# Attention and a quantised FFN on one core: key units on pairs of PSUM banks, another order at both ends of the loop, and seven blocks at once in the down stage

## What is computed

```python
x = x + xattn(_layernorm(x), ctx, ctx, mask, Wq, Wk, Wv, Wo)
    # q, k = rope(x Wq), rope(ctx Wk); logits = 30 tanh(q k * 0.0884 / 30); softmax; (w v) Wo
x = x + ffn(_layernorm(x), w1, w2, w3)
    # w -> NF4_CODE[searchsorted(bounds, w / absmax)] * absmax; (silu(x w1') * (x w2')) w3'
```

## Time and profile before

| | us |
|---|---|
| median of 3 runs (856.88 to 857.13) | 856.96 |
| profiled execution | 855.72 |
| span of its trace | 853.9 |
| TensorE busy | 803.7 |
| VectorE busy | 684.7 |
| GpSimd busy | 497.8 |
| ScalarE busy | 465.5 |
| mean granted clock of TensorE | 0.982 |

### The profile page before, as it was taken

One profiled execution on the slowest core, in us unless ns is written; L12 is line 12 of the kernel. 1 busy time (PEld: TensorE's weight loads), 2 busy tenths in 40 slices (PEclk: granted clock), 3 DMA queues, 4 the chain that ended last, 5 costly groups with the idle time before them and its releaser, 6 DMA issues.

```text
span 853.9 us, 10691 instructions
## 1 busy us (share of the span) xinstructions
PE 803.7 (94%) x3806; PEld 644.9 (76%) x3806; DVE 684.7 (80%) x745; ACT 465.5 (55%) x571; POOL 497.8 (58%) x270
## 2 busy tenths in 40 slices
PE   6798997999999999999999999998879999995998
PEld 4677885777788778877787778776668788884886
DVE  3876862589989899989989889889858999999512
ACT  5014752665665765665666656656325686866410
POOL 2545154776985986978977978967200344544100
PEclk9999998999999999999999999999999999997999
DMA  9676646432343433442533533412301121302112
GB/s 330 192 196 185 188 102 188 133 99 75 109 132 75 125 116 87 124 120 71 167 87 77 157 83 96 132 38 72 108 0 50 50 93 50 117 26 59 55 35 99
DMA packets 63541, 91.76 MB, mean 107 GB/s; under 512 B 6784, under 2 KB 30464, under 8 KB 63488
## 3 DMA queue, kind: packets, MB, share of 16 engines
q1 hardware_dynamic: 62304, 88.25, 35.7%
q10 hardware_dynamic: 1184, 2.82, 0.9%
HBM read 51.00 MB, written 19.07 MB: 82 GB/s over the span
## 4 chain that ended last, share of the span: by engine, by line
PE 81%; DVE 11%; issue 3%; DMA 2%; POOL 1%; ACT 1%; SPq 1%; DVEq 0%; POOLq 0%
PE bank L508 7%; PE bank L510 7%; PE bank L509 7%; PE bank L524 7%; PE bank L526 6%; PE bank L525 6%; PE avp L598 6%; PE bank L570 6%; PE bank L490 5%; PE bank L492 5%; PE bank L491 5%; PE trp L497 4%; DVE nfv L927 2%; PE bank L699 2%; PE bank L700 2%
## 5 line engine op out<-in xcount | busy, mean ns | idle before, releaser
L1247 POOL TENSOR_TENSOR eb<-eb,maskf 128x512 f32<-128x512 f32 x64 | 100.8, 1575 | 60.6 <-ACT eb L801 60.6
L799 ACT ACTIVATE eb<-bank 128x512 f32<-128x512 f32 x64 | 38.2, 597 | 177.6 <-PE bank L570 177.6
L1190 POOL TENSOR_TENSOR qT<-cs_loop,sw 128x512 f32<-128x512 f32 x57 | 101.9, 1787 | 34.8 <-DMA sw<-cs_loop 34.5
L508 PE MATMUL bank<-xh,wqh 128*128 128x512 f32 x256 | 106.5, 416 | 1.2 <-POOL wql L1181 1.2
L524 PE MATMUL bank<-woh,ath 128*128 128x512 f32 x256 | 107.6, 420 | 0.0
L526 PE MATMUL bank<-woh,atl 128*128 128x512 f32 x256 | 101.5, 396 | 0.0
L510 PE MATMUL bank<-xh,wql 128*128 128x512 f32 x256 | 101.5, 396 | 0.0
L525 PE MATMUL bank<-wol,ath 128*128 128x512 f32 x256 | 101.2, 395 | 0.0
L509 PE MATMUL bank<-xl,wqh 128*128 128x512 f32 x256 | 101.2, 395 | 0.0
L927 DVE SCALAR_TENSOR_TENSOR nfv<-nfq,nfv 128x1408 f32<-128x1408 uint8 x42 | 85.5, 2037 | 0.7
L935 DVE TENSOR_TENSOR cs_loop<-bank,csq 128x1024 f32<-128x1024 f32 x57 | 69.1, 1213 | 18.8 <-PE bank L510 18.8
(11 more groups left out here) (150 smaller groups left out, 1983.7 us busy)
## 6 DMA issues: line engine op xcount, KB each, us to landing
sw<-cs_loop SPq DMA_DIRECT2D x114, 128.0 KB, 2.3
stage<-wq_pieces SPq DMA_DIRECT2D x32, 256.0 KB, 3.0
stage<-wo_pieces SPq DMA_DIRECT2D x32, 256.0 KB, 2.8
stage<-dq_scratch SPq DMA_DIRECT2D x32, 256.0 KB, 3.6
sw<-cs_start SPq DMA_DIRECT2D x46, 128.0 KB, 2.3
ks_scratch<-qT SPq DMA_DIRECT2D x16, 256.0 KB, 2.5
vs_scratch<-vst SPq DMA_DIRECT2D x16, 256.0 KB, 3.2
kcur<-ks_scratch SPq DMA_DIRECT2D x16, 256.0 KB, 2.9
```

The lines of the kernel that those rows point to most:

```text
L508: nc.tensor.matmul(o, wqh[:, g, k, :], xh[:, k, cs], start=k == 0, stop=False)
L1190: nc.gpsimd.tensor_tensor(dst, products(ru, slot)[:, 0, :], sw[:, slot, :], ALU.add).then_inc(roped, 1)
```

## The change

The banks of `prj` become one tensor `prjs` of two banks. A key unit now writes the first bank of a pair, `prjs` or `avp` in turn. ScalarE copies its halves of 64 partitions crosswise into the second bank (`key_swap`), VectorE multiplies both banks by the two tables at once (`key_parts`), GpSimd subtracts (`key_rope`); SyncE sends no swaps for key units. The low parts of pieces 5 and 7 stand ahead of the first products on VectorE, those of 8 to 19 stand on GpSimd, and ScalarE's high parts stand between the copies.

SyncE issues the first four weight pieces of the loop during value units 14 and 15 and stores chunk 0 behind the loads of keys and values; ScalarE makes the first high part behind the tanh of step 1. From step 57 on `out_unit(j - 1)` stands ahead of the transposes of step j, and the work of the last head is spread anew over its steps. `nf_before` puts 122 places into the loop (116 before), 43 into the hidden units 0 to 19 (50 over all 22 before), and the rest behind the first pass of the down stage. In the down stage seven blocks go at once, into `lgp` too, so that the transposes of w3 have `trp` alone but for the second; one block follows.

```diff
+        key_pair = [prjs, avp]
...
-        FIRST_POOL = (0, 3, 6, 8, 10, 16, 18, 20, 22, 24, 26)
+        FIRST_POOL = (0, 3, 6, *range(8, 20), 20, 22, 24, 26)
...
             if slot <= NSTEP:
-                return 2 * min(max(0, slot - 2), 58)
+                return 122 * min(max(0, slot - 2), 58) // 58
             if slot <= NSTEP + 2 * HT:
-                return 116 + 50 * (slot - NSTEP) // (2 * HT)
-            return min(166 + 2 * (slot - NSTEP - 2 * HT), 16 * 11)
+                return 122 + min(43 * (slot - NSTEP) // 20, 43)
+            return min(165 + 2 * (slot - NSTEP - 2 * HT), 16 * 11)
...
+            def key_swap(u):
+
+                act.wait_ge(proj_done, u + 1)
+                pair = key_pair[u % 2]
+                nc.scalar.activation(pair[0:64, 1, :], pair[64:128, 0, :], ACT.Copy)
+                nc.scalar.activation(pair[64:128, 1, :], pair[0:64, 0, :], ACT.Copy).then_inc(key_swapped, 1)
...
+            def key_parts(u):
+
+                dve.wait_ge(key_swapped, u + 1)
+                wait(dve, roped, u - 1)
...
+                    key_pair[u % 2][:, :, :].rearrange("p c (b t) -> p c b t", b=4),
...
-            for n in (0, 3, 6):
+            for n in (0, 3, 6, 8):
                 first_low(n)
...
-                rope(u, u % 2, qT[:, u % 8 // 4, u % 4, :])
-                for n in {0: (8,), 2: (10,), 12: (16,), 13: (18,)}.get(u, ()):
-                    first_low(n)
-                if u == 5:
+                key_rope(u, qT[:, u % 8 // 4, u % 4, :])
+                if u < 7:
+                    first_low(u + 9)
+                if u == 7:
                     power(0, range(B))
+                if 11 <= u < 15:
+                    first_low(u + 5)
...
+                if v >= 14:
+                    head_piece(2 * v - 28)
+                    head_piece(2 * v - 27)
...
             weights(0)
+            weights(1)
             high(32)
-            weights(1)
...
+                    alone = j + AHEAD >= NUNIT
+                    if alone:
+                        out_unit(j - 1)
+                    if last and b in (3, 4):
+                        weight_transposes(b - 3)
+                    if last and b in (5, 7):
+                        token_transposes(b - 5)
+                        token_transposes(b - 4)
                     pe.wait_ge(an_done, j + 1)
...
-                    if j > 0:
+                    if j > 0 and not alone:
                         out_unit(j - 1)
...
-                for b in range(6):
+                for b in range(7):
+                    if n == 0 and b == 6:
+                        pe.wait_ge(wt_lo, 2 * HT + 2)
                     last = down(b, n, outs[b])
...
+                if n == 2 * HT - 1:
+                    down_hi(0)
...
-                for c, i in nf_adds(NSTEP + 2 * HT + n):
+                for c, i in nf_adds(NSTEP + 2 * HT + n - 1) if n > 0 else ():
                     nf_add(c, i)
```

205 lines of the change are left out of this document (108 added, 97 removed).

## The result

| | kernel before | changed kernel |
|---|---|---|
| median of the runs, us | 857.05 (856.88 to 858.10) | 830.35 (829.30 to 830.96) |
| span of the profiled execution, us | 853.9 | 828.9 |
| mean granted clock over the span | 0.982 | 0.994 |

The ratio is 0.9685, with a 95% interval of 0.9668 to 0.9701: 3.15% faster, 26.7 us. The forecast was 832.2 us in a range of 821 to 843.

What follows compares the result with a forecast made beforehand. TensorE was taken as the bound, busy 803.7 of 853.9 us, leaving about 39 idle us to win. Terms -7.5, -3.7, -7.4, -11.2 and +5.0 make -24.8: span 829.1, median 832.2 us, range 821 to 843.

Steps and rivals of the forecast that it cites:

- The sum: Whole kernel: five terms, -7.5 - 3.7 - 7.4 - 11.2 + 5.0, give -24.8 us on the profiled span.
- the steady loop: Loop from 152.3 to 580 us, where TensorE is never idle: nothing to gain, with 2 us as a bound for added adds.
- Key units: Key units up to the value stage: ScalarE copies replace the DMAs, value stage near 61.6 instead of 69.11, -7.5 us.
- The chain of a bank pair: Key units: a pair of banks is held 5.45 us against 5.46 TensorE needs for two units, so it just fits.
- the new wait of unit 8 on piece 15: Key unit 8: TensorE waits about 3.1 us for piece 15's low part on GpSimd, with 1.5 of half clock behind.
- The price of the copies: Key units: two ScalarE copies cost 1.09 us, bounds 1.0 and 2.4; rival of dear copies, 841 us, chance 0.10.
- Entry: Entry of the loop: earlier weight pieces and conversion behind the tanh start the unit at 147.0 instead of 152.30, -3.7 us.
- Loop's end: Last seven steps: output product ahead of transposes and spread layer norm start the first gate product near 629.7, -7.4 us.
- each after a wait of 0.9 to 1.6, under the limit of the clock: Loop's end: output products of steps 57 on wait only 0.9 to 1.6 us, so the clock doesn't fall.
- Gap: Before the down stage: no adds in the last two hidden units, start at 775.1 instead of 783.86, -11.2 us with clock.
- New wait in the down stage: Down stage: later last adds delay piece 8 to 814.5, wanted at 811.2; +3.3 us and +1.7 half clock, +5.0.
- the one on waits and the clock: Every TensorE wait: no loss of clock up to 1.8 us, a loss from about 2.

Runs made afterwards that it cites:

- low32_first: Changed kernel with GpSimd making the low part of piece 32, the first new query weight, ahead of the dequantization's multiply; 827.41 us, ratio 0.9639 to the kernel before.
- third_add_55: Changed kernel with the dequantization's places rounded otherwise, so a third add falls at step 55 and not at step 59; 828.26 us, ratio 0.9650 to the kernel before.
- places_before_b: Changed kernel with the dequantization's places as in the kernel before (116 in the loop, 50 in the feed-forward stage); 836.12 us, ratio 0.9741 to the kernel before.
- keys_alone_b: Kernel before with only the key units' part of the change (paired banks, two ScalarE copies, new order); 850.27 us, ratio 0.9914 to the kernel before.
- the last kernel: Changed kernel with piece 32's low part earlier, third add at step 55, 44 feed-forward places, piece 11's low part on VectorE, mask tables over two units; 816.42 us.
- low15_on_dve: Changed kernel with the low part of context piece 15 made on VectorE behind key unit 5, not on GpSimd; 829.62 us, ratio 0.9665 to the kernel before.

## Why the prediction was right, and where its steps were off

The sum was -24.8 us on the span and the measured one is -25.0. Where the waits would stand, and on what, is borne out below, but that the sum hits to 0.2 us is luck: the terms are off by +0.8, -0.3, +0.9, +0.2 and -2.2, and the steady loop, put at nothing, by +0.4. Of the -2.2, 1.7 are a half clock that stayed away in this execution and came in five of the six others that have the same wait.

**Key units, -7.5 said, -6.7 measured.** The chain of a bank pair (5.45 us for 5.46) was right, as the run with a third copy shows, and so was the new wait of unit 8 on piece 15. Two things were not in the walk. The operations on the mask tables, which I had costed at nothing, slow down beside GpSimd and make unit 6 wait 1.15 us:

```profile
22.95 1.09 DVE L998 TENSOR_TENSOR maskf<-maskf,nomask 128x128 f32<-128x128 f32 x1
23.95 1.38 DVE L999 TENSOR_TENSOR csq<-tab,keep 128x128 f32<-128x128 f32 x1
```

so unit 8 started 1.0 us later than said (34.89 for 33.9). And the units with transposes, 10 to 15, take 20.4 us together (42.04 to 62.47), where 2.73 + 0.36 + 0.1 for each makes 19.1: another 1.3, 0.4 of it one wait for VectorE's products. So the value stage started 2.4 us later than said (63.99 for 61.6). On the other side its first wait is 1.52 and not 2.02, and the half clock behind it went, 1.6 us that I had not counted. The price of the copies, for which I had bounds of 1.0 and 2.4 us, came out at 1.15. The rule of the Trainium skill (ScalarE: Activation LUTs, Step-by-step: what each stage is for), that ScalarE writes PSUM faster than SBUF, is borne out by 0.01 us only in the run with a third copy: 0.57 against 0.58 for the same shape.

**Entry, -3.7 said, -4.0 measured.** The wait was forecast at 2.9 us on GpSimd's order multiply, then low part; it is 2.57, and low32_first shows that order to be its whole cause. Of the gain, 2.7 us are SyncE's earlier issue.

**Loop's end, -7.4 said, -6.5 measured.** Less the 10.3 us won before it, my starts of the output products are 582.8, 589.0, 596.8, 603.2, 609.2 and 614.2; measured are 583.00, 589.16, 597.05, 604.00, 609.88 and 614.79. The walk was right to 0.3 us up to the third add. The step that failed is "each after a wait of 0.9 to 1.6, under the limit of the clock": the third add made it 2.24, and the clock fell. My own numbers had it: 599.3 to 607.1 is 7.8 us for a round that I had put at 4.85 on TensorE, which leaves a wait of up to 2.95. In third_add_55, without that add, neither the wait nor the fall is there.

**Gap, -11.2 said, -11.0 measured.** The wait is 1.14 us, the clock stays, and places_before_b brings both back.

**New wait in the down stage, +5.0 said, +2.8 measured.** The wait was sized 3.3 and is 2.47: the last add ended at 788.65 and the piece was there at 797.49, 8.8 us later, where I had 9.8. The half clock behind it, which I had charged with 1.7, did not come in this execution. That is not a size but a rule of mine that failed, the one on waits and the clock (last section).

## What to carry to other kernels

A wait taken away uncovers the next engine's queue, so walk that queue before choosing where the work goes: here each of the four new waits hung on one instruction in the wrong place (a low part behind a multiply, a third add, a low part behind a rope, an add one pass late). Moving three of them paid the wait and the clock behind it (4.2, 3.8 and 2.7 us, the last without any loss of clock to win back). The fourth was handed to the other engine, and such work must go where that engine idles in the trace: a subtraction of 128x512 gave 2.2 of 3.6 us behind unit 5, next to nothing there together with a table's operations, and as part of an order that relieves GpSimd three units earlier the 3.7 us that were forecast. When a block more is computed at once, ask what it covers; the work is the same.

## What the runs showed of the hardware

**The length of a wait alone doesn't decide whether the clock falls.** I had read a limit between 1.8 and 2.0 us out of the earlier trace rows. The trace of before already held a case against it, which I overlooked: TensorE's third long wait near the loop's end, of 2.09 us, has a clock of 1.00 behind it. In keys_alone_b, which is the kernel before at this place, the same wait of 2.09 us at 627.46 has 0.66 over the next 5 us.

```profile
633.85 0.66 PE L497 MATMUL trp<-tab,nrm 128*128 128x128 f32 x4 [2.09 <-DVE nrm L1066]
634.00:637.00 3.00, 3.00 (x16) 2.53 (x16) 0.69 (x1) 1.95 (x2) 0.00 (x0) 1.00 0.00 0
```

The same waits recur in these runs with the same instructions before and behind them. Key unit 8's wait of 2.35 us: in six runs the 5 us behind it have a granted clock of 0.66 to 0.70, in three 1.00. Query unit 8's of 2.57 us: 0.66 in seven runs, 1.00 in one. The output product's of 2.20 to 2.24 us: 0.66 in five, 1.00 in two. The ninth transposes' of 2.44 to 2.61 us: 0.66 to 0.72 in five, 1.00 in two. Three windows behind key unit 8, of the runs with 44 places, with six blocks and with the output product behind, which are the same program up to there:

```profile
35.20:40.20 5.00, 5.00 (x15) 3.97 (x16) 2.26 (x12) 0.39 (x1) 2.92 (x2) 0.66 0.33 123
35.10:40.10 5.00, 5.00 (x22) 4.14 (x23) 3.04 (x13) 1.14 (x2) 2.93 (x2) 1.00 0.33 123
34.90:39.90 5.00, 5.00 (x22) 4.15 (x23) 3.05 (x13) 1.14 (x2) 2.93 (x2) 1.00 0.39 123
```

The traces of both kernels and of the twelve experiments hold 107 waits of TensorE of 0.85 to 1.8 us. The clock over the 5 us behind them is 1.00, but for one of 0.94, where the next wait, of 4.4 us, begins 1.2 us later. Behind waits of 2.86 us and more it fell each time, by different amounts: to 0.66 after 2.86 and 3.13 us, 0.66 and 0.70 after 3.8, 0.50 after 3.86, 3.97 and 4.38 (2.5 us lost), 0.58 and 0.63 after 5.8 and 6.4, and after the gap of 10.0 us to 0.50 in two runs and 0.67 in that of the keys alone. The first matmul of a span, some 6 us behind its start, is the exception: it has 1.00 in all fourteen. Between 2.0 and 2.6 us the same wait went both ways, and no run shows what decides it. So a wait there costs itself and, mostly, something on top. What, the distances between two fixed points show, in runs with the fall against runs without: 1.4 to 1.6 us at key unit 8 (to the value stage), 0.9 to 1.5 at query unit 8 (to the first waiting output product), 1.0 at the output product (to the first gate product), 1.3 to 1.6 at the ninth transposes (to the end). Two executions of one kernel can so differ by some 5 us in four such places, an estimate from these distances. The four runs of the changed kernel lie within 1.7 us, those of places_before_b within 4.2, and those of the last kernel, which has no wait between 2.0 and 2.6 us, within 0.3. A distance between two points of the trace, with the clock looked up in both, says more on an edit than two spans do.

**Small operations of VectorE beside GpSimd.** A 128x128 multiply that takes 0.28 us alone took 1.38, and a 128x512 subtraction of 0.69 took 1.78 to 1.82 while GpSimd ran its own of 1.3. The multiply from 23.95 to 25.33 ran beside a subtraction of GpSimd from 23.84 to 25.19; the subtraction of low15_on_dve from 28.35 to 30.17 beside one from 28.32 to 29.62. Each started behind GpSimd's instruction and ended 0.14 and 0.55 us behind its end, so such an operation is better costed at the rest of the other engine's instruction with up to its own size on top. The reverse is seen in the last kernel: VectorE's subtraction from 19.45 to 20.13 took its 0.68 us, and GpSimd's sum, which started 0.16 us later, 1.67 instead of 1.29. Not every operation is hit: VectorE's products out of PSUM kept 1.22 us at 26.89 beside a sum of GpSimd from 26.75 on, and so did the statistics behind them.
